# Two-headed offsets in row groups of 64 ahead of the transposed scores of a local-attention block

## What is computed

```python
for l in range(2):                                   # DEPTH
    h = shift_token(x)
    q, k, v = split(h @ wqkv[l])                     # 8 heads of 64
    q, k = rotary_xpos(l2norm(q) * qs[l], l2norm(k) * ks[l])
    sim = einsum('bhwid,bhwjd->bhwij', q * 8, k)     # windows of 64, each sees itself and the one before
    sim = where((i < j) | (i > j + 64), -max, sim)
    o = einsum('bhwij,bhwjd->bhwid', softmax(sim), v)
    x = x + o @ wo[l]
    h = layernorm(shift_token(x)) * lg[l] + lb[l]
    a, g = split(h @ w1[l] + b1[l])
    x = x + (a * gelu(g)) @ w2[l] + b2[l]
```

## Time and profile before

| | |
|---|---|
| median of 3 runs | 2594.16 us |
| the profiled execution | 2591.7 us, span from first to last instruction 2589.9 us |
| TensorE busy in the span | 2277.1 us, 88% |
| VectorE, ScalarE, GpSimd busy | 1718.9, 1463.9, 1089.9 us |
| TensorE clock, mean granted | 0.957 of full speed |
| a round with `x_mean` | 25.45 us (from 299.76 to 325.21 us) |
| a round without it | 24.31 us (from 646.57 to 670.88 us) |

### The profile page before, as it was taken

The page is one execution under the profiler, slowest core; times in us unless marked ns, Lnnn a source line. Parts: engine busy times, 40 slices in busy tenths (PEclk is TensorE's granted clock), DMA queues, the critical chain, the costliest instruction groups (busy, mean ns, idle before and its releaser), DMA issues. The chain is left out here.

```text
span 2589.9 us, 52641 instructions
## 1 busy us (share of the span) xinstructions
PE 2277.1 (88%) x21574; PEld 1715.4 (66%) x21574; DVE 1718.9 (66%) x2800; ACT 1463.9 (57%) x2382; POOL 1089.9 (42%) x800
## 2 busy tenths in 40 slices
PE   2799999999999779999789999999999984878576
PEld 1577777777777556666457777777777753766266
DVE  3677777777777457777367777777877844533544
ACT  0567676666666425556456767666666642434332
POOL 4655555565565100000065555556556504410432
PEclk8899999999999889999989999999999987999899
DMA  7000000089999000000000000000000012110013
GB/s 147 1 1 1 2 2 1 1 91 115 108 122 109 8 1 2 2 2 2 1 1 2 1 1 2 2 2 1 2 2 2 1 54 60 56 53 1 29 51 99
DMA packets 185425, 73.63 MB, mean 28 GB/s; under 512 B 79658, under 2 KB 181204, under 8 KB 185060
## 3 DMA queue, kind: packets, MB, share of 16 engines
q1 hardware_dynamic: 177172, 56.68, 18.3%
q0 software_dynamic: 5568, 10.12, 1.3%
q10 hardware_dynamic: 2448, 3.48, 0.6%
HBM read 24.05 MB, written 46.18 MB: 27 GB/s over the span
## 5 line engine op out<-in xcount | busy, mean ns | idle before, releaser
L466 POOL TENSOR_TENSOR work<-work,rot_tables 128x512 f32<-128x512 f32 x256 | 446.9, 1767 | 451.3 <-ACT work L565 451.3
L474 POOL TENSOR_TENSOR work<-work 128x1024 f32<-128x1024 f32 x128 | 305.2, 2385 | 13.0 <-DVE work L884 3.1
L884 DVE TENSOR_TENSOR work<-work,rot_tables 128x1024 f32<-128x1024 f32 x128 | 163.9, 1281 | 112.1 <-ACT work L565 112.1
L1039 DVE TENSOR_REDUCE small<-psum 128x4 f32<-128x1024 f32 x128 | 156.6, 1223 | 91.1 <-PE psum L1545 91.0
L1273 PE MATMUL psum<-qkv_w_hi,h_hi 128*128 128x512 f32 x384 | 182.8, 476 | 18.8 <-POOL h_lo L493 16.3
L1425 PE MATMUL psum<-centered,ffn_w 128*128 128x256 f32 x768 | 191.1, 400 | 6.5 <-DVE centered L943 2.9
L901 DVE TENSOR_TENSOR work<-work,small 128x1024 f32<-128x1024 f32 x128 | 159.6, 1249 | 51.2 <-ACT small L579 47.0
L676 ACT ACTIVATE work<-psum 128x1024 f32<-128x1024 f32 x128 | 131.1, 1024 | 100.5 <-PE psum L1552 100.5
L481 POOL TENSOR_TENSOR y_all<-centered,squared 64x256 f32<-64x256 f32 x64 | 48.3, 755 | 308.2 <-ACT squared L625 305.6
L1363 PE MATMUL psum<-work 64*128 64x128 f32 (+1 forms) x2048 | 175.8, 311 | 0.0
L1425 PEld LDWEIGHTS psum<-centered,ffn_w 128*128 128x128 f32 x768 | 146.2, 197 | 37.4 <-DVE centered L943 18.7
(11 more groups left out here) (280 smaller groups left out, 5695.2 us busy)
## 6 DMA issues: line engine op xcount, KB each, us to landing
h_area<-mean_weights SPq DMA_DIRECT2D x16, 2048.0 KB, 27.2
tile_x<-h_area SPq DMA_DIRECT2D x78, 64.5 KB
work<-y_tokens SPq DMA_DIRECT2D x8, 512.0 KB, 6.1
stage<-in_consts ACTq DMA_DIRECT2D x1, 3009.0 KB, 12.7
work<-in_x SPq DMA_DIRECT2D x4, 512.0 KB, 28.3
expert_w<-in_ew SPq DMA_DIRECT2D x1, 2048.0 KB
expert_w<-in_ew SPq DMA_DIRECT2D x8, 256.0 KB
out<-work SPq DMA_DIRECT2D x8, 256.0 KB, 3.5
```

The costliest lines, as they stand in the source:

```text
L466: last = pool.tensor_tensor(b[:, :, :, o_], a[:, :, :, i_], tab[:, l, 1, t, :, o_].unsqueeze(2).to_broadcast([P, 2, HEADS, 32]), ALU.mult)
L474: pool.tensor_tensor(rC[:, t, :], rC[:, t, :], rB[:, t, :], ALU.add).then_inc(f_sum, 1)
L884: dve.tensor_tensor(g(rC[:, t, :]), g(rA[:, t, :]), tab[:, l, 0, t, :, :].unsqueeze(2).to_broadcast([P, 2, HEADS, DH]), ALU.mult)\
L1039: dve.tensor_reduce(dst, PS[:, 0:2, :].rearrange("p b (t j) -> p b t j", t=TILES), AX, ALU.max, negate=True).then_inc(a_smax, 1)
```

## The change

Three things are changed. First, the maxima are written twice: `mneg` becomes 128 columns for each tile, with the high and low parts at columns 0 to 15 and again at 64 to 79, and zero elsewhere; `m_T` multiplies with all 128 columns and `m_out` copies all 128 partitions, so that `mT` has the maxima in both halves. Second, `sel` has the ones of even heads in the rows h and h + 8 and those of odd heads 64 rows further down, and the offsets of a head are a product over the 64 rows of its half alone. Third, the order in `scores_T`: the masks alone (`bands`) open the banks, and the offsets of a group stand directly ahead of its products; the wait for `mT` comes after the masks of groups 0 and 1.

```diff
     for h in range(HEADS):
-        sel[h, h] = sel[h + HEADS, h] = 1.0
+        r = 64 * (h % 2)
+        sel[r + h, h] = sel[r + h + HEADS, h] = 1.0
-        mneg = sb("m_neg", [P, TILES, 2 * HEADS], BF16)
+        mneg = sb("m_neg", [P, TILES, P], BF16)
-            link(dve.memset(mT[:, :], 0.0))
+            link(dve.memset(mneg[:, :, :], 0.0))
                 def m_split(i):
-                    link(dve.tensor_copy(mneg[:, :, 0:HEADS], mx))
-                    dve.tensor_tensor(mneg[:, :, HEADS:2 * HEADS], mx, mneg[:, :, 0:HEADS], ALU.subtract)\
+                    twice = lambda a: a.unsqueeze(2).to_broadcast([P, TILES, 2, HEADS])
+                    mn = mneg[:, :, :].rearrange("p t (g r) -> p t g r", g=2)
+                    link(dve.tensor_copy(mn[:, :, :, 0:HEADS], twice(mx)))
+                    dve.tensor_tensor(mn[:, :, :, HEADS:2 * HEADS], twice(mx), mn[:, :, :, 0:HEADS], ALU.subtract)\
                         .then_inc(f_mlo, 1)
                 def m_out(i):
-                    dve.tensor_copy(mT[0:2 * HEADS, :], PS[0:2 * HEADS, 7, 0:T]).then_inc(f_mTs, 1)
+                    dve.tensor_copy(mT[:, :], PS[:, 7, 0:T]).then_inc(f_mTs, 1)
     # m_T
-                        last = pe.matmul(PS[0:2 * HEADS, 7, t * P:(t + 1) * P], mneg[:, t, :], eyeb[:, :],
+                        last = pe.matmul(PS[:, 7, t * P:(t + 1) * P], mneg[:, t, :], eyeb[:, :],
     # scores_T
-                    def offsets(bs, hs, w, j, i0, m):
+                    def bands(bs, hs, w, j, i0, m):
                         q = len(hs) // 2
                         for b in bs:
-                            for u in range(q):
-                                pe.matmul(PS[:, b, u * w:(u + 1) * w], sel[:, hs[0] + 2 * u + bs.index(b), :],
-                                          mT[:, i0:i0 + w], start=u == 0, stop=False, skip_group_check=True)
                             pe.matmul(PS[:, b, 0:q * w], eyeb[:, :], m.unsqueeze(1).to_broadcast([P, q, w]),
+                                      start=True, stop=False, skip_group_check=True)
+
+                    def products(bs, hs, w, j, i0, m):
+                        rows_ = lambda h: slice(64 * (h % 2), 64 * (h % 2) + 64)
+                        for h in hs:
+                            o = (h - hs[0]) // 2 * w
+                            pe.matmul(PS[:, bs[h % 2], o:o + w], sel[rows_(h), h, :], mT[rows_(h), i0:i0 + w],
                                       start=False, stop=False, skip_group_check=True)
...
+                    pe.wait_ge(f_cp, min(2 * i + 4, 2 * ITEMS * (f + 1)))
+                    bands(*groups[0])
+                    pe.wait_ge(f_vsb, min(i + 2, ITEMS * (f + 1)))
+                    bands(*groups[1])
                     pe.wait_ge(f_mTs, i + 1)
-                    pe.wait_ge(f_cp, min(2 * i + 4, 2 * ITEMS * (f + 1)))
-                    offsets(*groups[0])
-                    pe.wait_ge(f_vsb, min(i + 2, ITEMS * (f + 1)))
-                    offsets(*groups[1])
                     products(*groups[0])
                     products(*groups[1])
                     free(pe, f_u, i)
-                    offsets(*groups[2])
+                    bands(*groups[2])
                     products(*groups[2])
```

More of the change, by code:

```diff
@@ L1358, in offsets @@
                                       start=False, stop=False, skip_group_check=True)
-                    def products(bs, hs, w, j, i0, m):
                         for h in hs:
-                            r, o = slice(64 * (h % 2), 64 * (h % 2) + 64), (h - hs[0]) // 2 * w
-                            last = pe.matmul(PS[:, bs[h % 2], o:o + w], kT[r, h // 2, j * P:(j + 1) * P],
-                                             qT[r, h // 2, i0:i0 + w], start=False, stop=True, skip_group_check=True)
+                            o = (h - hs[0]) // 2 * w
@@ L1365, in products @@
+                            last = pe.matmul(PS[:, bs[h % 2], o:o + w], kT[rows_(h), h // 2, j * P:(j + 1) * P],
+                                             qT[rows_(h), h // 2, i0:i0 + w], start=False, stop=True, skip_group_check=True)
                         last.then_inc(f_st, 1)
+                    pe.wait_ge(f_cp, min(2 * i + 4, 2 * ITEMS * (f + 1)))
+                    bands(*groups[0])
+                    pe.wait_ge(f_vsb, min(i + 2, ITEMS * (f + 1)))
+                    bands(*groups[1])
```

## The result

The kernel after takes 2562.8 us (median of 4 runs, 2560.18 to 2567.91), the kernel before 2593.07 us beside it: ratio 0.989, 95% interval 0.9866 to 0.9914, faster by about 30 us. Measured again later, beside other runs of before, it was 0.9902 (0.9879 to 0.9925).

What follows compares the result with a forecast made beforehand. TensorE's order of work was taken to bound rounds, with VectorE's gated almost as late in 34 of 64. Savings of 28 x 0.495, 34 x 0.275 and 2 x 0.52 gave 24.3 us, so 2570 us, range 2560 to 2590.

Steps and rivals of the forecast that it cites:

- The offsets in halves: Offsets in pairs on TensorE: 0.77 us becomes 0.385 in groups 0 and 1, 0.33 becomes 0.165 in group 2.
- it doesn't do what it says: Rival: small offsets of the two halves run in turn, about 0.05 us lost a round, 2597 us; chance 0.04.
- The changes of type: Inside the 64-row form in scores_T: 0.08 us for each of three to fp32, 0.04 for the one back.
- The forecast's own range: 2563 to 2577 us, with changes of type between 0.03 and 0.12 us each.
- The wait for `gated`: Ahead of group 2: without x_mean it can come only 0.09 us earlier, 0.275 saved; with x_mean slack 0.48.
- `m_split`, `m_T`, `m_out`: Wider maxima: m_split 0.025 us longer, delaying up, in full only with x_mean; m_T and m_out cost nothing.
- The rule of the Trainium skill: Weights load under a running matmul only over different row groups; first weights not hidden at type changes, 21.5 us saved.
- What is late next: With x_mean, attend has 0.72 us of slack for group 1's exponentials against 0.495 saved; without, gated limits group 2.
- the second rival: A further wait caps rounds with x_mean too, so all save 0.275 us: 17.6 us, 2577; chance 0.12.
- Slower by emptying at each change of type: Rival: 64-row form emptied at four type changes, 0.26 us each, 0.265 us lost a round, 2611 us; chance 0.06.

Runs made afterwards that it cites:

- e10: Kernel after, offsets of even heads issued twice and those of odd heads left out, so all run in one half: 0.9994 of before.
- e1: Kernel before with only the maxima written twice, product and copy at full width, offsets unchanged: 1.0009 of before.
- e6: Kernel before with one more GELU of 256 columns a round on ScalarE, so gated ends later: 1.0035 of before.
- e7: Kernel after with the same extra GELU a round on ScalarE: 0.9967 of before.
- e8: Kernel after with ScalarE's square of the second tile behind the GELU, its sums behind gated and x_center: 0.9876 of before.
- e2: Kernel after, but offsets over all 128 rows at their new place, order without halves: 2610.41 us, 1.0095 of before.
- e3: Kernel after, but offsets in halves at their old place ahead of their group's mask, halves without the order: 0.9979 of before.
- e5: Kernel after, but a group's offsets issued first for its even heads, then for its odd heads: 0.9901 of before.
- e4: Kernel after, but offsets of groups 0 and 1 together ahead of both groups' products, two changes of type fewer: 0.9903 of before.
- e9: Kernel after with the edits of e4 and e8 together: 2556.66 us, 0.9875 of before.

## Why the prediction was right, point by point

- **Forecast and measurement.** 2570 us forecast, 2562.8 measured, in the range of 2560 to 2590; both sides by their own run of before, 24 us less against 30 less. Signs and mechanism held, the gain was undersized by a fifth.
- **The offsets in halves.** Forecast 0.385 and 0.165 saved, as two halves at the same time. In e10 the same offsets in one half make groups 0 and 1 0.385 and group 2 0.16 us longer. The pairs start 0.003 us apart, not 0.08. The rival "it doesn't do what it says" is refuted.
- **The changes of type: the term that was mis-sized.** I took 0.08 for each to fp32 and 0.04 back, 0.28 in all. The single records show 0.03, 0.05 and 0.03 for the three to fp32 and nothing for the one back, 0.11 in all. The reason I gave, the 0.10 of the first weights with "a little of it" under the offsets, was right but for the "little": most of it is covered. By the same columns, ways in and ways out, groups 0 and 1 should take 2.845 us without changes and took 2.97, group 2 1.335 and took 1.38: together 0.17, so another 0.06 lies in the ways in and the columns, which I had rounded. With `x_mean` the saving ahead of `down` was therefore 0.63 and not 0.52. Against the 0.495 a round that I summed, 0.60 arrived (mean of 26 rounds: 25.47 to 24.87); the 0.03 between is what e1 shows. 28 such rounds make 3 us of the missing 6. The forecast's own range had 2563 us for changes of 0.03.
- **The wait for `gated`.** Forecast: 0.09 us of slack without `x_mean`, then bound. Measured: group 2 starts 0.12 us earlier after `m_T` (6.40 to 6.28), 0.06 behind the end of `gated`. The slack was 0.10, and `gated` comes 0.02 earlier after `m_T`, as it does in e1, which fits `m_T` itself coming later. With the 0.23 of group 2 and that 0.02 taken off again, 0.34 a round arrives, against 0.275 forecast. 34 rounds make 2 us. By rounds the gain is then 28 x 0.60 + 34 x 0.34 and some 1 us for the two last: 29.7 of the 30 measured. e6 and e7 confirm both slacks of the kernel before, 0.10 and over 0.36 (0.48 forecast), and both of the kernel after.
- **`m_split`, `m_T`, `m_out`.** Forecast 0.025 us for the first and nothing for the others. e1's rounds with `x_mean` are 0.03 longer: the size was right. The place was not: `up` did not move after `m_T`, the time is lost ahead of `m_T`. The cast still ends with GpSimd's sum: in the round shown, the sum ends at 295.66 and the cast at 295.71. In both traces it ends 0.03 to 0.05 us behind the sum in all rounds but the first and the last of each run, and in the last, with no sum beside it, it takes 0.18 us instead of 0.48 to 0.58. So the explanation of its length stands.
- **The rule of the Trainium skill** ("TensorE: Matmul & The Clock Gate", section "The mechanism") that weights load under a running matmul only over other rows gave 21.5 us, the trace's own pricing 24.3, and 30 were measured. The trace after contradicts the strict rule directly: the weights of the first fp32 product are loaded from 300.398 on, and the offset over the same rows runs from 300.397 to the product's start at 300.479.
- **What is late next.** `attend` was forecast to have room for 0.495 us with `x_mean`; it had room for 0.63 (it starts 9.30 us after `m_T`; the exponentials of group 1 end at about 9.13). In e8, 0.28 more in the other rounds were too much for it. So the second rival, a further wait that caps the rounds with `x_mean`, was not true of this change; a wait of its kind stands at the next one.
- **Slower by emptying at each change of type:** it would need 0.19 us a change; four cost 0.11 to 0.17 together. The cost is real at a change of form: 0.09 to 0.10 us each way in e2 and e3, and 0.10 more when an fp32 product comes first. That rival had the price of another event.

## What to carry to other kernels

A product over few rows saves time only if the other half of the array has work in the same stretch, and most of that only if it stands among products of the same form: here the halves alone brought 0.2%, the place alone lost 1%, and the two together won 1.1%. Before sizing a gain on the busiest engine, look for the waits whose slack is smaller than the gain; where an engine's stretches of work are counted in tenths of a microsecond, 0.1 us of slack at one semaphore decides how much of it arrives. A delay of the suspected releaser, in both kernels, measures that slack directly, and the starts of the single records in the trace say where an advance arrives.

## What the runs showed of the hardware that was not expected

- Products for the two halves need not be issued in turn: four for one half and then four for the other took as long as alternating ones (e5, within 0.02 us), and a product for the idle half started 0.08 us ahead of the offset that was issued before it (e10).
- A crossing from 128-row to 64-row products costs 0.09 to 0.10 us, and one back as much, for bfloat16 and fp32 alike. The first fp32 pair behind a crossing is 0.10 us longer than the next; behind bfloat16 products of the 64-row form only 0.03 to 0.05 of that is left, and from fp32 to bfloat16 nothing is lost.
- In seven traces, after (both), e4, e5, e7, e8 and e9, TensorE stands still for 0.3 to 1.9 us in the middle of `attend`, once or twice, in the first run of `ffn`; in before, e1, e2, e3, e6 and e10 it does not. The traces point to its own instructions coming late. Numbered by their start, the products and loads at which the 13 standstills end are number 9410, 9922, 13250 or 14274 in all seven, whole multiples of 256 apart. A queue of the kind "instruction" brings 173 packets of 16 KB, about one for each 256 of the 43148 records, and 11 of the 13 standstills end 1.1 to 1.7 us after one of them has landed (the others 2.7 and 3.7). In the seven traces the packet ahead of number 9922 lands when TensorE has at most 19 records left to that place, in the six others 75 or more; in the second run of `ffn` every packet lands with over 120 left. In the first run other transfers fill the DMA engines (a share of 1.20 from 575 to 582 us in after), in the second hardly any do. No run was made to test it, and the rounds alone don't decide it: e7's without `x_mean` are as long as those of before, and it stands still twice.
